# Attention on one Trainium2 core: the output products of every unit in one block of eight

## The reference

```python
xd = (x @ W_down).reshape(b, t, h, s)
keys = jnp.einsum('bthk,hik->bthi', xd, tokeys) * scale
queries = jnp.einsum('bthk,hik->bthi', xd, toqueries) * scale
values = jnp.einsum('bthk,hik->bthi', xd, tovalues)
dot = jnp.einsum('bqhs,bkhs->bhqk', queries, keys)
attn = jax.nn.softmax(dot, axis=-1)
out = jnp.einsum('bhqk,bkhs->bqhs', attn, values).reshape(b, t, e)
return out @ W_unify + b_unify
```

## Time and profile before

| | us |
|---|---|
| median of 3 runs | 3727.38 |
| the profiled execution | 3727.63 |
| its span in the trace | 3725.8 |
| attention, first exponential to last P | 418.8 to 2822 |
| of it with M: first to last reduction of scores | 424.7 to 2768.7 |
| of it without M, the last 24 units | 2768.7 to 2822 |

### The profile page before, as it was taken

How to read it: one execution, slowest core, us unless ns; L and a number is a source line. 1 busy time by engine, 2 the same in 40 slices (tenths; PEclk the granted TensorE clock), 3 DMA queues, 4 the chain that set the end, 5 groups by cost and what they waited for, 6 DMA issues and landing times. The chain is left out here.

```text
span 3725.8 us, 78041 instructions
## 1 busy us (share of the span) xinstructions
PE 3608.3 (97%) x31366; PEld 2064.9 (55%) x31366; DVE 3209.2 (86%) x4509; ACT 2643.1 (71%) x4951; POOL 369.9 (10%) x331
## 2 busy tenths in 40 slices
PE   8799899999999999999999999999998989999998
PEld 6487444444444444444444444444445668888887
DVE  6667799999999999999999999999975757766664
ACT  3455598989888989888999888999896442223332
POOL 0123200000000000000000000000002203403323
PEclk9899899999999999999999999999999999999999
DMA  4910322021122113112202202200012000122332
GB/s 139 249 38 18 113 23 30 4 30 26 7 23 22 17 10 34 18 9 24 29 4 30 26 7 24 32 6 7 4 32 82 34 2 29 55 93 66 82 85 39
DMA packets 299888, 149.50 MB, mean 40 GB/s; under 512 B 218527, under 2 KB 278057, under 8 KB 296980
## 3 DMA queue, kind: packets, MB, share of 16 engines
q1 hardware_dynamic: 287252, 133.97, 19.4%
q0 software_dynamic: 12288, 10.70, 1.7%
HBM read 86.46 MB, written 64.18 MB: 40 GB/s over the span
## 5 line engine op out<-in xcount | busy, mean ns | idle before, releaser
L1202 ACT ACTIVATE probs<-attention_scores_t_sums 128x512 f32<-128x512 f32 x4096 | 2142.2, 597 | 246.0 <-PE attention_scores_t_sums L1126 243.8
L1126 PE MATMUL attention_scores_t_sums<-q_operand,k_operand 50*128 50x512 f32 x2048 | 702.9, 443 | 15.4 <-ACTq L1216 13.8
L1120 PE MATMUL attention_scores_q_sums<-attention_k_operand,attention_q_operand 48*128 48x512 f32 x2048 | 699.8, 439 | 0.0
L1126 PE MATMUL attention_scores_t_sums<-attention_q_operand,attention_k_operand 50*128 50x512 f32 x2048 | 698.6, 443 | 0.0
L1120 PE MATMUL attention_scores_q_sums<-k_operand,q_operand 48*128 48x512 f32 x1952 | 669.6, 440 | 0.0
L1242 DVE TENSOR_REDUCE max_parts<-attention_scores_q_sums 128x1 f32<-128x512 f32 x1008 | 639.1, 670 | 1.6 <-PE attention_scores_q_sums L1120 1.6
L1242 DVE TENSOR_REDUCE attention_max_parts<-attention_scores_q_sums 128x1 f32<-128x512 f32 x992 | 628.9, 670 | 0.0
L1235 DVE TENSOR_REDUCE max_parts<-attention_scores_q_sums 128x2 f32<-128x1024 f32 x504 | 605.7, 1202 | 8.6 <-PE attention_scores_q_sums L1120 8.5
L1136 PE MATMUL attention_o_psum_sums<-probs,attention_v_heads 128*32 128x256 f32 x8208 | 602.8, 388 | 0.0
L1136 PE MATMUL attention_o_psum_sums<-probs,v_heads 128*32 128x256 f32 x8192 | 602.1, 388 | 0.0
L1235 DVE TENSOR_REDUCE attention_max_parts<-attention_scores_q_sums 128x2 f32<-128x1024 f32 x496 | 596.8, 1203 | 0.0
(11 more groups left out here) (330 smaller groups left out, 4687.7 us busy)
## 6 DMA issues: line engine op xcount, KB each, us to landing
expert_rows<-attention_empty_rows SPq DMA_DIRECT2D x16, 516.0 KB, 5.6
v_scratch<-value_chunk SPq DMA_DIRECT2D x16, 512.0 KB, 5.4
w_whole<-in_L_ffn_ew SPq DMA_DIRECT2D x8, 1024.0 KB, 7.3
experts_w_whole<-in_L_ffn_ew SPq DMA_DIRECT2D x8, 1024.0 KB, 5.7
q_operand<-q_scratch SPq DMA_DIRECT2D x24, 256.0 KB, 4.7
k_operand<-k_scratch SPq DMA_DIRECT2D x24, 256.0 KB, 6.4
attention_q_operand<-q_scratch SPq DMA_DIRECT2D x24, 256.0 KB, 4.8
attention_k_operand<-k_scratch SPq DMA_DIRECT2D x24, 256.0 KB, 6.5
```

Of the source, the lines that this page charges most:

```text
L1120: nc.tensor.matmul(SA[:, (2 * h + j) * CH:(2 * h + j + 1) * CH], QOP[b][64 * h:64 * h + ROWS, qt * P:(qt + 1) * P], KOP[b][64 * h:64 * h + ...
L1126: nc.tensor.matmul(ST[bank_n][:, :], KOP[b][64 * h:64 * h + ROWS + 2, kt * P:(kt + 1) * P], QOP[b][64 * h:64 * h + ROWS + 2, c * CH:(c + 1 ...
L1202: nc.scalar.activation(PR[:, tile, :], ST[bank_n][:, :], ACT.Exp).then_inc(st_free, 1)
```

## The change

Even units had two blocks of four products, behind pair 2 and behind pair 4; odd units had one block of eight behind pair 3. Now an even unit has one block of eight behind pair 2. Odd units stay as they were. The products, their order and their operands are the same.

```diff
@@ -974,7 +974,7 @@
         recip_out = sem("recip_den_out")
         block = ph.block()
         LOAD = 12 * 16
-        BLOCKS = ({(0, 1): (0,), (1, 1): (1,)}, {(1, 0): (0, 1)})
+        BLOCKS = ({(0, 1): (0, 1)}, {(1, 0): (0, 1)})
 
         def bank(r, u, t):
             return (FIRST + r * ROUND + 4 * u + t) % NB
```

## The result

The changed kernel takes 3908.63 us (median of four runs, 3906.33 to 3910.21), the kernel before, run beside it, 3727.43 us. The ratio is 1.0483, with an interval of 1.0467 to 1.0500: slower by 181 us.

What follows compares the result with a forecast made beforehand. VectorE was taken to bound at 4.65 us for two units; a 5.03 bank loop over 500 pairs gives +190, net +176 with M, +3 without: +179 on 3727.6, about 3906 us. Range of 8 in 10: 3845 to 3950.

Steps and rivals of the forecast that it cites:

- a loop of 5.03 us for two units: Attention with M: three banks for T make TensorE wait for exponentials; 1.70 + 0.43 + 1.00 + 0.90 + 1.00.
- VectorE's bound before: Attention with M, kernel before: VectorE's reductions set the pace at 4.65 us for two units, TensorE close behind at 4.60.
- TensorE's own time: TensorE's order without bank waits: 4.60 us for two units before, 4.28 after, with 1.38 for the stretch of five pairs.
- The 1.70 over the banks: Pair 3 (even) to pair 3 (odd), over two exponentials: 0.56 + 0.49 + 0.60 + 0.05 = 1.70 us.
- 0.43 and not 0.33 behind a T that waited: Step from a T held by its bank to the next block: 0.43 us, against 0.33 in the running order.
- The once-a-round work: VectorE's work beside the pairs: some 14 of 19 us fall into its spare time; ScalarE's copy of the sums costs 0.
- the +3 for the units without M: End of attention, 12 pairs of units: loop 4.87 against 4.57 before gives +4 us, taken as +3.
- the third rival: Same loop plus 19 us or more from the round's copy, or T2's own wait, 50 us; chance 0.04 above 3962.
- The first rival: Banks don't hold TensorE up, VectorE stays at 4.65, only the end gains 4 us: 3724 us; chance 0.06.
- The second: Only VectorE is starved, at pair 3 of even units, 0.02 late each time: 10 us, 3738 us; chance 0.04.
- A block's own price of 0.14: TensorE's blocks: two of four take 1.14, one of eight 1.00, so 0.14 us goes with a block, not its products.
- the rule that spoke the other way: A tiling mode change drains TensorE; the change removes a third of the switches between pairs and products, so less work.

Runs made afterwards that it cites:

- short_exp: Changed kernel with exponentials over 256 of their 512 columns, the skipped half filled ahead of attention: 3737.02 us.
- half_before_3b: Kernel before with M tiles over 256 of their 512 keys, still three banks for T: 3675.55 us.
- four_fours: Changed kernel with blocks of four behind pairs 2 and 4 in every unit instead of blocks of eight: 3862.43 us.
- half_both3_4b: Changed kernel with the block of eight behind pair 3 in every unit, M tiles over half of the keys and a fourth bank for T: 3448.24 us.
- both_pair3: Changed kernel with the block of eight behind pair 3 in every unit, full M tiles, three banks for T: 4055.68 us.
- half_both3_3b: Changed kernel with the block of eight behind pair 3 in every unit, M tiles over half of the keys, three banks for T: 4030.38 us.

## Why the prediction was right

It said about 3906 us, by a loop of 5.03 us for two units; 3908.63 was measured, with a loop of 5.03 to 5.04. The mechanism was right too: T2 and T3 (odd) are held by the banks in every pair of units, a shorter exponential takes the loss away, and a fourth bank takes most of it away.

- **VectorE's bound before.** short_exp bears it out: TensorE's order is another, of 4.28 by the prediction's sum, and the pace is the same as before, with VectorE busy all the time. half_before_3b, 54 us faster than the kernel beside it, does not test it, since smaller M tiles shorten TensorE's order too and the banks held that kernel up.
- **TensorE's own time.** 0.90 and 1.00 were measured as said. The stretch of five pairs can't be seen without its wait, so its 1.38 is not shown as a whole; its start has the steps that were said (1507.49, 1507.82, 1508.06), and four_fours (4.92 said, 4 x 1.23 found) confirms the 0.57 of a short block and the 0.66 of two pairs.
- **The 1.70 over the banks.** From pair 3 at 1507.49 to T3 at 1509.19: 1.70. short_exp shows that ScalarE's time is in it, the fourth bank (225 us) that the banks are.
- **0.43 and not 0.33 behind a T that waited.** 1509.19 to 1509.62: 0.43. The other end of this term would have given 50 us less.
- **The once-a-round work.** 176 us were said for the part with M and 176 measured; 3 for the part without, 2.7 measured. The copy of the sums, costed at nothing, adds 0.05 us on average to a pair of units that holds it, some 3 us in all.
- **Two terms that were off without weight.** M1 (odd) was put 1.67 behind the even block's start; by the prediction's own steps it is 1.00 + 0.33 + 0.24 = 1.57, and 1.58 was measured (1506.48 to 1508.06). F's end leaves room for that. And the +3 for the units without M was right for a reason that the trace turns round. Behind the odd block, T4 and the next T1 read different halves of the partitions (`64 * h`) and start together (both at 2966.12 in one unit), while T2, on the same half as T1, follows 0.34 later. The stretch is then 0.67 and not 0.74 (2966.12 to 2966.78), and the exponential starts 0.53 behind its T and not 0.56: 4.76 us for two units where 4.87 was said.
- **What was not said.** The 3.3 us more ahead of attention. They are not the change's: over the kernels above, short_exp left aside, the first exponential starts between 418.3 and 422.1 us, with no order in it. Waits of T were put at some 500; they are 1057, because T2 (odd) waits too. Its wait in the trace is the one that the third rival named, but the wait of T3 ends later and covers it, which is why it costs nothing.
- **What was a little off.** VectorE's busy share fell to 96.3%, and I had said 93%. Its records have grown a little (R 0.69 us for 0.67, F 1.21 for 1.20 in the median), by 4 x 0.017 + 2 x 0.012 = 0.09 us for two units. That is 1.8 of the 3.3 points by which I was off. The rest is overlap: a reduction's record runs on into the next one's when the two follow at once. In the part with M, such overlap sums to 221 us before and to 176 after, and the 45 us are 1.8 points of 2519. So VectorE's busy share, too, says more than its work.
- **The first rival** (not slower) failed by the loop. **The second** (10 us, VectorE starved) can't be told apart beneath it in this run; short_exp, where VectorE's work and the place of the block are those of the changed kernel and the pace is within 0.002 us of before, leaves it no more than about 1 us.

A block's own price of 0.14, beside its products, is borne out by four_fours, whose extra block and shorter stretches cost what the sum said. With such a price at every change between pairs and products, the trace agrees with the rule that spoke the other way, the drain at a change of tiling mode (the Trainium skill, "TensorEngine Tiling (Array Packing)", Key Properties); that a drain is what costs it, no run shows. It was outweighed, not wrong: by the prediction's terms the new order saves TensorE 0.32 for two units and adds 0.65 and 0.10 of waiting. Of the 0.43 more, 0.05 fill the distance up to VectorE's 4.65, and 0.38 are left.

## What to carry to other kernels

With n buffers between two engines, measure how long one buffer's way round takes (fill, wait, use, release), and ask of every stretch of the producer's order with n + 1 fills or more what covers that time. In this case each such stretch with full exponentials had a held fill in it, with three banks and with four. The reverse does not hold: half_before_3b was held up with three fills in a stretch at most, half_both3_4b with four fills on four banks. Short blocks of other work between the fills look like overhead and may be the cover; so the best order depends on the number of buffers, and the two are to be tried together: the same order was the slowest on three banks and the fastest on four. An engine that is shown as 97% busy before and after can hide a loss of 5%; the distance between like instructions doesn't.

## What the hardware showed that I had not expected

In both_pair3 and half_both3_3b, TensorE's granted clock fell to half, that is from 2.4 to 1.2 GHz, in the last units, those without M (both_pair3, then half_both3_3b; columns as in the first section):

```profile
3075.00:3090.00 15.00, 12.54 (x120) 5.21 (x119) 0.00 (x0) 11.74 (x24) 0.00 (x0) 1.00 0.19 7
...
3110.00:3146.00 36.00, 33.72 (x197) 12.31 (x193) 0.00 (x0) 17.20 (x33) 3.60 (x2) 0.53 0.02 6
```

```profile
3050.00:3070.00 20.00, 18.70 (x102) 6.56 (x100) 0.00 (x0) 10.38 (x20) 0.00 (x0) 0.50 0.02 3
```

Ahead of it, in those units, TensorE was busy for 12.54 of 15.00 us in both_pair3: it stood still for a sixth of the time, for the banks and with no M to fill in. Once the clock was down, a block of eight took 1.86 us in place of 1.00:

```profile
3115.82 1.94 PE L1136 MATMUL attention_o_psum_sums<-probs,attention_v_heads 128*32 128x256 f32 x16
3117.68 1.22 PE L1126 MATMUL attention_scores_t_sums<-attention_q_operand,attention_k_operand 50*128 50x512 f32 x3
```

In the same units the changed kernel was busy for 54.02 of 56.30 us and kept 1.00 to the end of attention, and the kernel before for all of 53.6. both_pair3's four executions come in the order of their mean granted clock: 4048.35 us at 0.985, 4050.65 at 0.983, 4060.71 at 0.980 and 4067.14 at 0.978. This suggests that a wait on a buffer can cost twice, by itself and by the clock. It is not shown: no run here changes the waits of these units alone.
